# Turned halves of queries and keys stored by GpSimd in two transfers, and the order of work around units 50 to 59 changed

## The reference, cut to what matters

```python
x = x + attn(layernorm(x))         # 32 query heads, 8 key/value heads, head size 128
x = x + matmul(fake_quant(layernorm(x)), fake_quant(ctx))
x = x + experts(layernorm(x))      # router, top 16 of 64, rank 8
# attn, for each sequence and head:
q, k = rope(h @ Wq), rope(h @ Wk)  # rope: q * cos + rotate_half(q) * sin
p = softmax(causal(q @ k.T / sqrt(128)))
out = concat(p @ v) @ Wo
```

## Time and profile before

| | |
|---|---|
| device time, three runs | 1272.68, 1273.97, 1274.65 us (median 1273.97) |
| profiled execution: time, span | 1273.53 us, 1271.8 us |
| PE busy | 1248.8 us (98% of the span) |
| DVE, ACT, POOL busy | 850.8 (67%), 787.3 (62%), 611.8 us (48%) |
| PE's granted clock | 1.00 in every slice |
| PE busy in 400 to 500, 700 to 800, 800 to 900 us | 100.00, 93.73, 97.55 us |

### The profile page before, as it was taken

How to read it: one execution, slowest core, us unless ns; L and a number is a source line. 1 busy time by engine, 2 the same in 40 slices (tenths; PEclk the granted TensorE clock), 3 DMA queues, 4 the chain that set the end, 5 groups by cost and what they waited for, 6 DMA issues and landing times. The chain is left out here.

```text
span 1271.8 us, 19740 instructions
## 1 busy us (share of the span) xinstructions
PE 1248.8 (98%) x6831; PEld 1073.2 (84%) x6831; DVE 850.8 (67%) x1919; ACT 787.3 (62%) x1601; POOL 611.8 (48%) x450
## 2 busy tenths in 40 slices
PE   9999999999999999999999998999999999999998
PEld 8898898888888888888888887878888888868787
DVE  7874735566666667666666766655786777988863
ACT  6412247677767777777777878873333367766530
POOL 4776766678767877778677755520000000021100
PEclk9999999999999999999999999999999999999999
DMA  8043144454857958649486588759964567401111
GB/s 281 18 138 128 59 158 158 148 167 140 240 151 209 247 166 237 170 119 229 142 228 178 129 227 266 210 186 269 294 186 129 165 207 258 147 3 34 50 43 50
DMA packets 122402, 208.72 MB, mean 164 GB/s; under 512 B 15408, under 2 KB 56368, under 8 KB 118720
## 3 DMA queue, kind: packets, MB, share of 16 engines
q1 hardware_dynamic: 118272, 178.10, 42.9%
q0 software_dynamic: 4032, 29.36, 12.2%
HBM read 147.40 MB, written 88.08 MB: 185 GB/s over the span
## 5 line engine op out<-in xcount | busy, mean ns | idle before, releaser
L1342 DVE TENSOR_TENSOR pT_lo<-banks,pT_hi 128x512 fp32r<-128x512 f32 (+1 forms) x192 | 103.6, 595 | 116.0 <-ACT pT_hi L1048 116.0
L1791 PE MATMUL banks<-ob_hi,oa_hi 128*128 128x512 f32 x384 | 149.4, 389 | 0.0
L1791 PE MATMUL banks<-ob_lo,oa_hi 128*128 128x512 f32 x384 | 149.4, 389 | 0.0
L1791 PE MATMUL banks<-ob_hi,oa_lo 128*128 128x512 f32 x384 | 149.4, 389 | 0.0
L1749 PE MATMUL banks<-xc,nring_hi_a 128*128 128x512 f32 x448 | 138.5, 390 | 0.7 <-DVE q_made L1283 0.3
L1749 PE MATMUL banks<-xc,nring_hi_b 128*128 128x512 f32 x448 | 138.6, 391 | 0.0
L1032 ACT CAST oa_hi<-oraw 128x1024 fp32r<-128x1024 f32 x48 | 50.4, 1051 | 127.0 <-PE banks L1791 116.3
L2006 POOL TENSOR_TENSOR resid<-resid,colterm 128x1024 f32<-128x1024 f32 x8 | 19.9, 2491 | 205.4 <-ACT colterm L2064 132.6
L1048 ACT CAST pT_hi<-banks 128x512 fp32r<-128x512 f32 (+1 forms) x192 | 86.5, 527 | 44.8 <-PE banks L1714 44.1
L1697 PE MATMUL banks<-kT,q_hi 128*128 128x512 f32 (+2 forms) x384 | 104.2, 352 | 0.0
L775 POOL TENSOR_TENSOR q_lo<-q_raw,q_hi 128x512 fp32r<-128x512 f32 x64 | 88.9, 1390 | 30.3 <-ACT q_hi L986 30.2
(11 more groups left out here) (275 smaller groups left out, 3405.1 us busy)
## 6 DMA issues: line engine op xcount, KB each, us to landing
q_raw<-qk_dram SPq DMA_DIRECT2D x64, 256.0 KB, 3.9
o_S<-o_st SPq DMA_DIRECT2D x64, 256.0 KB, 3.2
w<-in_L_attn_Wo SPq DMA_DIRECT2D x32, 512.0 KB, 6.4
oraw<-o_S SPq DMA_DIRECT2D x32, 512.0 KB, 4.1
nraw<-in_L_attn_Wq SPq DMA_DIRECT2D x28, 512.0 KB, 6.2
o_S<-o_S POOLq DMA_DIRECT2D x12, 1024.0 KB, 9.7
o_S<-o_N POOLq DMA_DIRECT2D x12, 1024.0 KB, 10.3
resid<-in_x SPq DMA_DIRECT2D x16, 512.0 KB, 7.0
```

The lines of the kernel that those rows point to most:

```text
L1342: nc.vector.tensor_tensor(pT[1][:, sl], turned_chunk(turned, mixed, c), as32(pT[0][:, sl]), ALU.subtract).then_inc(pT_lo, 1)
L1791: ins = nc.tensor.matmul(step_bank(m, t), oa[a][:, s % 2, k, t * P:(t + 1) * P], ob[c][:, s % 2, k, :], start=(q == 0 and k == 0 and i == ...
```

## The change

Five edits:

1. The turned halves are stored by POOL (`keep_turned`, now called at the end of `turn_added`) in two transfers for each sequence, where SP had four. Each takes 128 partitions of 512 numbers. In DRAM it writes two blocks of 64 rows, one in each head. Every count of `q_kept` is halved.
2. `oraw` has four buffers of half size in the first steps. `load_first(f)` waits for the low half of step `f - 4`. Steps 1 to 3 are loaded in unit 56, the later ones a unit earlier.
3. The queries of eight units (52 to 57, 59, 60) are loaded an iteration earlier, as soon as their buffer is free, in front of `keep_out`. The stores that stood between are gone from SP.
4. In units 50 and 52 (`HALVED`) PE does `mix(u - 1)` between the two halves of the unit's job. In unit 56 DVE's first addition of the last job stands ahead of `add_pair`.
5. At the start of the last stage one turn of quantised rows, one of `A_w` and the second product change places on PE; ACT and DVE follow.

```diff
+SOONER = LAST_JOB_UNIT - 4
+HALVED = [u for u in SHORT if u % 2 == 0 and u < LAST_JOB_UNIT]
+    def first_rows(f):
+        return oraw[:, f % 4 // 2, :, (f % 2) * 256:(f % 2) * 256 + 256]
...
-        def keep_turned(j):
-            ...
-            sp.wait_ge(turn_made, 2 * e + b + 1)
-            for n, (x, y) in enumerate(((0, 1), (1, 0))):
-                rows = slice(64 * n, 64 * n + 64)
-                sp.dma_start(qk_dram[head + n, b, 64 * x:64 * x + 64], made_half(b, 0)[rows, :]).then_inc(q_kept[b], 16)
-                sp.dma_start(qk_dram[head + n, b, 64 * y:64 * y + 64], made_half(b, 1)[rows, :]).then_inc(q_kept[b], 16)
+        qk_halves = qk_dram.rearrange("h b (x r) c -> (h b x) r c", r=64)
+        def keep_turned(e, b):
+            head = narrow_head(e)[2]
+            pool.wait_ge(turn_made, 2 * e + b + 1)
+            first = 4 * head + 2 * b
+            for i, halves in enumerate((slice(first, first + 6, 5), slice(first + 1, first + 5, 3))):
+                nc.gpsimd.dma_start(out=qk_halves[halves], in_=made_half(b, i)).then_inc(q_kept[b], 16)
...
-            if f < 2:
-                sp.wait_ge(job_read, 6 * NARROW - 1 + f)
-            if f >= 2:
-                sp.wait_ge(fa_lo, f - 1)
+            if f < 4:
+                sp.wait_ge(job_read, 6 * NARROW - 1 + f // 2)
+            if f >= 4:
+                sp.wait_ge(fa_lo, f - 3)
...
+        def whole_early(v):
+            return SOONER <= v < UNITS and (v - 4, 0) in JOB_AT and turning_job(v) <= JOB_AT[v - 4, 0]
...
-                load_q(u + 2)
+            late = u + 2 < UNITS and not whole_early(u + 2)
...
+            if whole_early(u + 3):
+                load_q(u + 3)
...
+            if u == LAST_JOB_UNIT:
+                begin_last(JOBS - 1)
             if 0 < u <= PAIRED and u % 2 == 0:
                 add_pair(u - 1)
...
-            place(u, 0)
-            if u > 0:
-                mix(u - 1)
-            place(u, 1)
+            if u in HALVED:
+                job(JOB_AT[u, 0], range(KH // 2))
+                mix(u - 1)
+                job(JOB_AT[u, 0], range(KH // 2, KH))
+            else:
+                ...
...
         turn_fill("k", 0)
+        turn_fill("a", 4)
+        turn_quantised(2)
         multiply(1)
-        turn_fill("a", 4)
         router_matrix()
-        turn_fills("a", range(5, 7))
-        turn_quantised(2)
-        turn_fill("a", 7)
+        turn_fills("a", range(5, 8))
```

More of the change, by code:

```diff
@@ L331, in attention @@
     w00_in, w10_in, w01_in = ([sem(f"w{n}_in{q}") for q in range(2)] for n in ("00", "10", "01"))
-    o_in = [sem(f"o_in{n}") for n in range(2)]
+    o_in = [sem(f"o_in{n}") for n in range(4)]
     fa_hi, fb_hi, fa_lo, fb_lo = sem("fa_hi"), sem("fb_hi"), sem("fa_lo"), sem("fb_lo")
@@ L652, in _ @@
                 load_narrow(1)
+        def whole_early(v):
+            return SOONER <= v < UNITS and (v - 4, 0) in JOB_AT and turning_job(v) <= JOB_AT[v - 4, 0]
         early = 0
         for u in range(1, UNITS):
-            tight = u + 2 < UNITS and (u - 1, 0) in JOB_AT and JOB_AT[u - 1, 0] == turning_job(u + 2)
-            if u + 2 < UNITS and not tight:
+            late = u + 2 < UNITS and not whole_early(u + 2)
+            tight = late and (u - 1, 0) in JOB_AT and JOB_AT[u - 1, 0] == turning_job(u + 2)
+            if late and not tight:
                 load_q(u + 2)
@@ L673, in _ @@
                     load_narrow(j // 7 + 2)
+            if whole_early(u + 3):
+                load_q(u + 3)
             if u == LAST_JOB_UNIT:
-                load_first(1)
+                for f in range(1, 4):
+                    load_first(f)
             if 2 <= u <= LAST_JOB_UNIT + 1:
                 keep_out(u - 2)
[L678 to L682, removed]
+            if u > LAST_JOB_UNIT:
+                for f in steps_of(u + 2):
                     load_first(f)
@@ L840, in first_low @@
             pool.wait_ge(fa_hi, f + 1)
-            nc.gpsimd.tensor_tensor(oa[1][:, f % 2, :, 0:256], oraw[:, f % 2, :, 0:256],
+            nc.gpsimd.tensor_tensor(oa[1][:, f % 2, :, 0:256], first_rows(f),
                                     as32(oa[0][:, f % 2, :, 0:256]), ALU.subtract).then_inc(fa_lo, 1)
@@ L1012, in first_high @@
             if f == 1:
-                act.wait_ge(q_kept[0], 64 * NARROW)
+                act.wait_ge(q_kept[0], 32 * NARROW)
             if f >= 2:
                 act.wait_ge(first_done, f - 1)
-            nc.scalar.copy(oa[0][:, f % 2, :, 0:256], oraw[:, f % 2, :, 0:256]).then_inc(fa_hi, 1)
+            nc.scalar.copy(oa[0][:, f % 2, :, 0:256], first_rows(f)).then_inc(fa_hi, 1)
             act.wait_ge(w00_in[q // 4], 64)
@@ L1292, in begin_read, with begin_last @@
             nc.vector.tensor_tensor(n_u[:, 0, :], job_bank(j), n_u[:, 0, :], ALU.add)
+        def begin_last(j):
+            e, b = j // 7, job_bank(j)
+            dve.wait_ge(job_done, j + 1)
+            dve.wait_ge(job_read, 6 * e + 4)
+            dve.wait_ge(turn_made, 2 * e + 1)
+            link(nc.vector.tensor_tensor(b, b, n_u[:, 0, :], ALU.add))
         def read_job(j, begun=False):
@@ L1323, in read_job @@
             else:
-                dve.wait_ge(job_read, 6 * e + 4)
-                dve.wait_ge(turn_made, 2 * e + 1)
-                link(nc.vector.tensor_tensor(b, b, n_u[:, 0, :], ALU.add))
+                if not begun:
+                    begin_last(j)
                 job_turned(b, q_made[:, 0, :], q_made[:, 1, :])
@@ L1382, in keep_first_pass @@
             dve.wait_ge(first_done, PAIRS)
+            dve.wait_ge(q_kept[1], 32 * NARROW)
             for n in range(2):
@@ L1733, in mix, with job @@
             ins.then_inc(mix_done, 1)
-        def job(j):
+        def job(j, ks=range(KH)):
             e, i, p = j // 7, j % 7, SEQ[j % 7]
@@ L1746, in job @@
             opens = p in ("P1", "P6", "P5", "P3")
-            for k in range(KH):
+            for k in ks:
                 for n, (a, c) in enumerate(PASSES):
@@ L1751, in job @@
                                            skip_group_check=True)
-            ins.then_inc(job_done, 1)
+            if ks[-1] == KH - 1:
+                ins.then_inc(job_done, 1)
         def first_step(f):
@@ L2086, in _ @@
         high("k", 0)
+        high("a", 4)
+        copy_turned(2)
         scale_tile(3)
         root(0)
+        read_product(1)
         normalise(0)
-        high("a", 4)
-        read_product(1)
         act.wait_ge(mT_done, 1)
@@ L2094, in _ @@
         highs("a", range(5, 8))
-        copy_turned(2)
         highs("x", range(2))
@@ L2244, in _ @@
         lows("a", range(3))
+        quantise(2)
+        row_term(1)
         add_product(0)
-        product_stats(0)
         low("a", 3)
         low("k", 0)
+        product_stats(0)
+        low("a", 4)
         scale_of(0)
-        row_term(1)
-        quantise(2)
-        low("a", 4)
         low("a", 5)
```

34 lines of the change are left out of this document (14 added, 20 removed).

## The result

The changed kernel takes 1622.25 us (median of five runs, 1618.89 to 1623.4), the kernel before 1273.33 in the same comparison: a ratio of 1.273, interval 1.2713 to 1.2747. The forecast was 1269.7 us, in a range of 1267.2 to 1275.8. It was wrong by 353 us, and on the wrong side.

A forecast was written before the change was run, and what follows sets the result against it. PE, busy for 98% of the span, was taken as the bound, so only its waits could go. Gains of 0.95 + 0.90 + 0.65 + 1.8 = 4.3 us from 1273.53, plus 0.44, gave 1269.7 us, range 1267.2 to 1275.8.

The forecast's parts named there:

- the 0 for the stores: Moving the half-panel stores from SP to POOL: 0 gained or lost, with 0.80 us an issue and a landing of 2.6.
- Rival A: New stores land slowly on two engines, 8.5 us, delaying loads for units 50 and 58: +7.7, 1277.3 us; chance 0.15.
- A margin of 2.83 us for `q_lo`: In unit 53 `q_lo` ended 2.83 us ahead of its scores, so two POOL issues of 1.60 would fit.
- Rival B: POOL is late: an issue takes 2.0 us, not 0.80; units 51, 53, 57 lose 1.2 each, 1273.3 us; chance 0.10.
- The cover that I named for the stores: Slack for POOL's stores: the margin of 2.83 us before unit 53's scores, and a job's 2.72.
- HALVED: Mix half a job earlier: unit 50 falls from 8.55 to 7.59, 0.95 us gained (bounds 0.43, 0.95); unit 52 gains 0.
- Earlier queries: ACT's wait for unit 55's queries goes: unit 54 gains 0.90 us, the next turn interval 0.65; units 56 and 57 0.
- Four buffers: Four `oraw` buffers end ACT's two waits between 760 and 860 us: 1.8 us gained at unit 58 (bounds 1.46, 2.14).
- Last stage: Reordered work where PE waits 1.25 us for `wT_lo`: 0 taken, bounds 0 and 1.25 gained.
- the sum of 4.3: Total gain forecast in us: 0.95 + 0.90 + 0.65 + 1.8, with the stores and the last stage at 0.

The follow-up runs named there:

- pool_flat: The changed kernel with its two GpSimd stores of a half-panel each writing 128 rows of DRAM that follow one another, not two blocks; 1272.12 us, ratio 0.9992.
- rest_first: SyncE's four stores and edits 2 to 5, with the load of first step 1 moved right behind that of step 0; 1269.3 us, ratio 0.9969.
- pool_four: The changed kernel with GpSimd storing each half-panel in four transfers of 64 partitions by 64 rows, not two of two blocks; 1277.28 us, ratio 1.002.
- pad_16: The changed kernel with its 64 GpSimd stores going to a scratch tensor in 16 blocks of 8 rows with gaps; 1272.64 us, ratio 0.9992.
- sp_four_rest: The changed kernel with the four SyncE stores of the kernel before, edits 2 to 5 kept; 1270.17 us, ratio 0.9977.

## Why the prediction was wrong

**The step that failed is the 0 for the stores, and in it two readings: the landing, and the missing wait at the issue.** "How a store of this new shape lands no row shows ... I take 2.6." It was 9.1. I took the nearest row, that of a store to one block, and it was not near even in its bytes: those stores are 128 KB, the new ones 256 KB, and 256 KB in one piece land in 3.6 us (`pool_flat`). The Trainium skill stood against it ("DMA: Bandwidth & Descriptors", "Why a DMA increments its semaphore by 16 and not by 1"), and the runs agree with its rule: two engines at two blocks, sixteen at sixteen. Rival A, worked out from it, had 8.5 us. I gave it 0.15, partly for the exception that the section makes for some direct copies issued by software; by the DMA share of 0.14 these stores do not fall under it. "Nothing of before shows a transfer held to two" was no argument, since no transfer of before had such a shape.

**The missing wait is nearly all of the loss: rival A itself was 345 us short.** It priced a late landing at two loads only, 7.7 us. It had no term for the queue: "one issue on POOL takes 0.80" is right for the issue, but the next store of the kind can't leave before the last has moved. A margin of 2.83 us for `q_lo` met more than 8 us of POOL standing at each pair of stores, in every panel and not only in the three units I looked at. Rival B had the place right (PE waits for `q_lo` and `nring_lo`) and the mechanism wrong: not the length of the issue but the time in front of it. The cover that I named for the stores was for 1.60 us; the question to ask was what an issue waits for if its predecessor is slow.

**HALVED**: the mechanism held, 0.74 for 0.95, within its bounds. Unit 52 did not move (8.72 to 8.76). **Earlier queries**: 0.91 and 0.66 for 0.90 and 0.65. **Four buffers**: 1.41 for 1.8, just under the lower bound of 1.46, and unit 57 gave 0.21 back; "neither wait for a DMA is left" was wrong, one of 1.91 us stayed, and with it gone (`rest_first`) unit 58 is 10.54, near the 10.31 of its upper bound. For unit 57 I had forecast nothing, and that it fell by 0.53 there shows that this load was part of its length. **Last stage**: PE's wait fell from 1.25 to 0.70, and from the first scores of unit 63 to the end the span went from 438.80 to 438.63: 0 was right.

So the sum of 4.3 for all but the stores was 3.5, and all but 0.8 us of the error lies in the one term that was put at zero.

**The stores at GpSimd brought nothing even in a good shape.** Beside SyncE's four stores with the same edits (1270.17 us, a gain of 0.23%), `pool_flat` took 1272.12 and `pool_four` 1277.28. The intervals of the first two overlap, that of `pool_four` is clear of both. In the profiled executions, 1272.4 and 1268.3 us long, most of what `pool_flat` loses is in unit 57, 15.56 us long and not 11.99, where PE waited 2.73 us for `ob_lo`. DVE and PE there:

```profile
770.84 4.09 DVE L1389 TENSOR_TENSOR ob_lo<-w,ob_hi 128x1024 fp32r<-128x1024 f32 x1
```

```profile
775.08 0.77 PE L1780 MATMUL banks<-ob_hi,oa_hi 128*128 128x512 f32 x1 [2.73 <-DVE ob_lo L1389]
775.64 0.63 PE L1780 MATMUL banks<-ob_lo,oa_hi 128*128 128x512 f32 x1
```

The wait costs more than its length: the matmuls behind it take 0.63 us and not 0.39, at a granted clock of 0.50 from 775.0 to 777.5 us. That the stores of GpSimd, one of which was issued at 770.77, lengthen the subtraction is argued from the place alone.

## What to carry to other kernels

Before two transfers are merged into one, look at the slowest dimension of both sides: 64 rows became 2 blocks, and sixteen engines became two. Then price a slow transfer three times: for what waits for it, for the next one on its queue, and for the other work of the queue and of its engines; here the first was put at 8 us, and the kernel lost some 345 us more. And where a rule speaks against a term put at zero and no row of the trace shows that shape, the rule's price is the nearer bound, and the nearest row of another shape is not.

## What the runs showed of the hardware

- The store held at the queue: on GpSimd's queue each of 48 held two-block stores left 0.26 to 0.40 us after the last one had landed, while an accumulate left 2.0 us behind such a store, and a store on sixteen engines 0.8 us behind it. With four blocks two stores were out at once and a further one was held.
- The hold is not proportional to the landing: with four blocks the landing is 6.5 us in place of 9.1, and POOL's idle time 36.0 us in place of 353.0.
- A DVE subtraction of 128x1024 (`ob_lo`) that began while GpSimd issued stores took 4.09 us (`pool_flat`), and 4.05 and 4.00 at the same place in two other runs with GpSimd stores (`pool_four`, `pad_16`); with SyncE's stores it took 1.48 (`sp_four_rest`). I saw this at one place of the program only, and did not isolate it.
- The granted clock of TensorE was 0.65 in the window from 249 to 257 us, in which it did no matmul, and 1.00 in the one from 286 to 293, in which it was busy; 1.00 is the level of 2.4 GHz, 0.65 a mean over both levels. The 71.5 us of longer matmuls come from that, and they go when the waits go (PE was busy for 1248.8 us in `sp_four_rest`, as in the kernel before).
